# A small U-shaped convolution net on sixteen 32x32 TensorE tiles, with its deconvolutions folded into the convolutions behind them

## The chip, the cores and the metric

The kernel runs on one core of a Trainium2 chip. The metric is the time of one launch in device microseconds, the median of three runs. Engines are called as the profile calls them: PE is TensorE's matmul, PEld its weight load, DVE is VectorE, ACT is ScalarE, POOL is GpSimd, SP is SyncE, whose only work here is to start transfers.

## The reference

`x` is 16 images of 32 channels, 128x128, fp32. Four layers follow, each `x = x + layer(group_norm(x))`; the first three (an attention-like layer, a deformable convolution with a state-space scan, a plain 3x3 convolution) are not touched. The fourth is a small net. Cut to what matters:

```python
y = get_operator(x)                    # five edge filters, 160 channels
y = maxpool2(conv3x3(y, conv1))        # 32 channels from here on; 64x64
y = maxpool2(conv3x3(y, conv2))        # 32x32
y = maxpool2(conv3x3(y, conv3))        # 16x16
y = conv3x3(y, conv4)
y = conv3x3(deconv2x2(y, deconv1), conv5)   # 32x32
y = conv3x3(deconv2x2(y, deconv2), conv6)   # 64x64
y = conv3x3(deconv2x2(y, deconv3), conv7)   # 128x128
return orig * y                             # orig = group_norm(x)
```

`deconv2x2` has stride 2 and a 2x2 kernel, so each input pixel makes a 2x2 block of its own; `conv3x3` pads with zeros and both add a bias. Up to `conv1`'s pooling is the function `edges`; everything behind it, and the product and sum with `x`, is the function `hourglass`, which alone is changed.

## The kernel before

`program` runs its stages one behind the other, each with its own tiles, semaphores and a barrier at its end: norm tables, the layers, `edges` (line names `l3a_`), and last `hourglass` (`l3b_`). `edges` writes `pooled` (32 channels of 64x64) to HBM.

`hourglass` takes four images at a time (`IM`), 32 channels of each, on the 128 partitions; so there are four groups (`NG`), a hardware loop. Weights are block-diagonal 128x128 matrices made on the host (`w_convs`, `w_deconvs`): three quarters of each is zeros. Within a group the layers run strictly in order on PE: `conv2` (8 chunks of 512 columns), `conv3` (2), `conv4` (2), `deconv1`, `conv5` (2), `deconv2` (8), `conv6` (8), `deconv3` (32), `conv7` (32). A convolution chunk is nine matmuls, one for each tap, into one of four PSUM banks (`convolve`, L2200); a deconvolution chunk is one matmul (`spread`, L2207, L2225). ACT adds the bias and scatters a deconvolution's product into the padded input of the next convolution (L2260, L2274); DVE pools (L2316), and for `conv7` multiplies by the normalised `x` and adds `x` (L2343, L2346). The normalised `x` is made by ACT from pieces of eight rows (L2302). Each piece of `x` is loaded by POOL's queue and stored by SP's. SP loads the next group's `in2` when the last `conv2` chunk of this group is done. The memsets of the six padded inputs are on DVE (L2309), and PE waits for all.

Of the kernel before, what the change touches and what calls it, by code (L numbers as in the profile page):

```python
# [5 lines left out]
ACT = mybir.ActivationFunctionType  # L6
ALU = mybir.AluOpType
AX = mybir.AxisListType
P = 128
# [2082 lines left out]
def hourglass(nc, x, table, first, w_convs, w_deconvs, biases, out, B):  # L2092
    IM = P // T
    NG = B // IM
    RO = 8
    NT = H // RO
    XB = 4
    BANKS = 4
    S1, S2, S3 = H // 2, H // 4, H // 8

    phases = (("conv2", S1 * S1 // 512, "v"), ("conv3", S2 * S2 // 512, "v"), ("conv4", 2, "a"), ("deconv1", 2, "a"),
              ("conv5", S2 * S2 // 512, "a"), ("deconv2", 4 * S3 * S3 * 4 // 512, "a"),
              ("conv6", S1 * S1 // 512, "a"), ("deconv3", 4 * S1 * S1 // 512, "a"), ("conv7", H * W // 512, "v"))
    first_chunk, engine_of = {}, []
    for name, n, engine in phases:
        first_chunk[name] = len(engine_of)
        engine_of += [engine] * n
    CHUNKS = len(engine_of)
    assert CHUNKS % BANKS == 0
    PRIMED = CHUNKS  # L2110
    taken_by = {"a": engine_of.count("a"), "v": engine_of.count("v")}

    def chunk_no(g, name, i=0):

        return g * CHUNKS + i + first_chunk[name]

    def taken_before(g, name, engine, i=0):

        return g * taken_by[engine] + i + engine_of[:first_chunk[name]].count(engine)

    with ExitStack() as ctx:
        m = Memory(nc, ctx, "l3b")
        wc = m.sb("wc", [P, 6, 9, P])
        wd = m.sb("wd", [P, 3, 4, P])
        bias = m.sb("bias", [P, 9])
        gn = m.sb("gn", [P, NG, 2])
        gcur = m.sb("gcur", [P, 2])

        in2 = m.sb("in2", [P, S1 + 2, S1 + 2])
        in3 = m.sb("in3", [P, S2 + 2, S2 + 2])  # L2130
        in4 = m.sb("in4", [P, S3 + 2, S3 + 2])
        in5 = m.sb("in5", [P, S2 + 2, S2 + 2])
        in6 = m.sb("in6", [P, S1 + 2, S1 + 2])
        in7 = m.sb("in7", [P, H + 2, W + 2])

        up1 = m.sb("up1", [P, S3, S3])
        up2 = m.sb("up2", [P, S2, S2])
        up3 = m.sb("up3", [P, S1, S1])
        most = m.sb("most", [P, S2, S2])
        xt = m.sb("xt", [P, XB, RO, W])  # L2140
        ht = m.sb("ht", [P, 2, RO, W])
        ps = m.bank("ps", BANKS)
        names = "w_load zeroed in2_load product_done act_took dve_took in3_ready in4_ready gcur_ready h_ready out_ready"
        (w_load, zeroed, in2_load, product_done, act_took, dve_took, in3_ready, in4_ready, gcur_ready, h_ready,
         out_ready) = (m.sem(n) for n in names.split())
        x_in = [m.sem(f"x_in{u}") for u in range(XB)]
        stored = [m.sem(f"stored{u}") for u in range(XB)]
        block = ctx.enter_context(nc.Block())
        group = lambda a: a.rearrange("(g b) c h w -> g (b c) (h w)", b=IM)
        xg, og, fg = group(x), group(out), group(first)  # L2150

        @block.sync
        def _(sp):
            for dst, src in ((wc[:], w_convs), (wd[:], w_deconvs), (bias[:], biases)):
                sp.dma_start(dst, src).then_inc(w_load, 16)
            tb = table.rearrange("(g b) (c q) s -> b c g q s", b=IM, q=4)
            for b in range(IM):
                sp.dma_start(gn[T * b:T * (b + 1), :, :], tb[b, :, :, 0, :]).then_inc(w_load, 16)
            sp.wait_ge(zeroed, 6)
            with sp.Fori(0, NG) as g:  # L2160

                sp.wait_ge(product_done, chunk_no(g, "conv3"))
                sp.dma_start(in2[:, 1:S1 + 1, 1:S1 + 1], fg[at(g), :, :].rearrange("g p (h w) -> (g p) h w", w=S1)).then_inc(in2_load, 16)
                with sp.Fori(0, NT // XB) as j:
                    for u in range(XB):
                        sp.wait_ge(out_ready, g * NT + j * XB + (u + 3))
                        sp.dma_start(og[at(g), :, at(RO * W * (j * XB + u), RO * W)].rearrange("g p n -> (g p) n"),  # L2167
                                     xt[:, u].rearrange("p y x -> p (y x)")).then_inc(stored[u], 16)
            for u in range(XB):
                sp.wait_ge(stored[u], 16 * (NG * NT // XB + 1))  # L2170

        @block.gpsimd
        def _(pool):
            with pool.Fori(0, NG) as g:
                with pool.Fori(0, NT // XB) as j:
                    for u in range(XB):
                        pool.wait_ge(stored[u], (g * (NT // XB) + j) * 16 + 16)
                        pool.dma_start(xt[:, u].rearrange("p y x -> p (y x)"),  # L2178
                                       xg[at(g), :, at(RO * W * (j * XB + u), RO * W)].rearrange("g p n -> (g p) n")).then_inc(x_in[u], 16)

        @block.tensor
        def _(pe):
            pe.wait_ge(w_load, 16 * (3 + IM))
            pe.wait_ge(zeroed, 6)

            def bank_free(g, name, i, u):

                engine = engine_of[first_chunk[name]]
                pe.wait_ge(act_took if engine == "a" else dve_took, taken_before(g, name, engine, i) + (u + 1))  # L2190

            def bank(name, u, n=512):
                first_column = 512 * ((first_chunk[name] + u) % BANKS)
                return ps[:, first_column:first_column + n]

            def convolve(g, name, k, src, size, rows, i, u):

                bank_free(g, name, i, u)
                for tap in range(9):
                    ins = pe.matmul(bank(name, u, rows * size), wc[:, k, tap, :],  # L2200
                                    src[:, at((i + u) * rows + tap // 3, rows), tap % 3:tap % 3 + size], start=tap == 0, stop=tap == 8)
                ins.then_inc(product_done, 1)

            def spread(g, name, k, src, rows, j, tap):

                bank_free(g, name, j * 4, tap)
                pe.matmul(bank(name, tap), wd[:, k, tap, :], src[:, at(j * rows, rows), :], start=True, stop=True).then_inc(product_done, 1)  # L2207

            with pe.Fori(0, NG) as g:
                with pe.Fori(0, S1 // 8 // BANKS) as j:  # L2210
                    pe.wait_ge(in2_load, g * 16 + 16)
                    for u in range(BANKS):
                        convolve(g, "conv2", 0, in2, S1, 512 // S1, j * BANKS, u)
                pe.wait_ge(in3_ready, g + 1)
                for u in range(2):
                    convolve(g, "conv3", 1, in3, S2, 512 // S2, 0, u)
                pe.wait_ge(in4_ready, g + 1)
                for u in range(2):
                    convolve(g, "conv4", 2, in4, S3, S3 // 2, 0, u)

                pe.wait_ge(act_took, taken_before(g, "deconv1", "a") + BANKS)
                for p in range(2):
                    bank_free(g, "deconv1", 0, p)
                    for q in range(2):
                        ins = pe.matmul(bank("deconv1", p)[:, S3 * S3 * q:S3 * S3 * (q + 1)], wd[:, 0, 2 * p + q, :],  # L2225
                                        up1[:, :, :].rearrange("p h w -> p (h w)"), start=True, stop=True)
                    ins.then_inc(product_done, 1)
                pe.wait_ge(act_took, taken_before(g, "conv5", "a") + BANKS)
                for u in range(2):
                    convolve(g, "conv5", 3, in5, S2, 512 // S2, 0, u)  # L2230
                pe.wait_ge(act_took, taken_before(g, "deconv2", "a") + BANKS)
                for j in range(2):
                    for tap in range(4):
                        spread(g, "deconv2", 1, up2, S2 // 2, j, tap)
                with pe.Fori(0, S1 // 8 // BANKS) as j:
                    pe.wait_ge(act_took, taken_before(g, "conv6", "a") + BANKS)
                    for u in range(BANKS):
                        convolve(g, "conv6", 4, in6, S1, 512 // S1, j * BANKS, u)
                with pe.Fori(0, S1 // 8) as j:
                    pe.wait_ge(act_took, taken_before(g, "deconv3", "a") + BANKS)  # L2240
                    for tap in range(4):
                        spread(g, "deconv3", 2, up3, 8, j, tap)
                with pe.Fori(0, H // 4 // BANKS) as j:
                    pe.wait_ge(act_took, taken_before(g, "conv7", "a") + BANKS)
                    for u in range(BANKS):
                        convolve(g, "conv7", 5, in7, W, 512 // W, j * BANKS, u)
# [324 lines left out]
```

## Time and profile before

| | us |
|---|---|
| timed runs | 25,470.23, 25,509.12, 25,365.6; median 25,470.23 |
| span of the profiled execution (the only time recorded of it) | 25,493.9 |
| PE busy in it | 20,717.4, 81% |
| `hourglass`, from the last work of `edges` to the end of the span | 23,568 to 25,494: 1,926 |
| of it before the first matmul | 49 |
| one group of four images | 473 |

The span is cut from the first to the last instruction. Matmuls are pipelined: a record lasts about 165 ns longer than the time until the next one can begin on the same part of the array, so spacings count and not durations.

### The profile page before, as it was taken

What the parts mean: (1) busy time and instruction counts of PE and PEld (TensorE: products, weight loads), DVE (VectorE), ACT (ScalarE), POOL (GpSimd) and SP (SyncE); (2) the same over time, 40 slices, a digit from 0 to 9 for tenths busy, and PEclk for the clock granted to TensorE, in tenths of its full rate; (3) what the DMA queues carried; (4) which work ended last, traced back from release to release, by engine and by line L of the source; (5) the groups of instructions that cost most, each with busy time, mean ns of one, the idle gap of its engine ahead of it and who ended that gap; (6) DMA issues with size and microseconds to landing.
All of it is one profiled execution on the core that took longest, in us unless ns stands there. A gap on an engine that the chain in (4) does not pass through costs nothing. (4 is left out here: it accounts for less than half of the span.)

```text
span 25493.9 us, 384771 instructions
## 1 busy us (share of the span) xinstructions
PE 20717.4 (81%) x134800; PEld 8220.3 (32%) x134800; DVE 15361.5 (60%) x15737; ACT 14120.3 (55%) x22694; POOL 9395.5 (37%) x7816
## 2 busy tenths in 40 slices
PE   6888888884368888888859999997348888888899
PEld 2333333331122222222225444454013333333344
DVE  8999999994167777777835555555133333333111
ACT  6999998994257777777636665665222222222111
POOL 6777777782057777777720010001000000000000
PEclk9999999997678888888877776777679999999999
DMA  1000000006810000000031111112960011001111
GB/s 63 12 12 12 12 12 12 12 12 127 155 47 17 17 18 16 18 18 16 16 79 26 28 33 28 26 28 62 193 149 22 22 29 26 22 22 27 39 38 44
DMA packets 1295345, 995.42 MB, mean 39 GB/s; under 512 B 742248, under 2 KB 1151440, under 8 KB 1258968
## 3 DMA queue, kind: packets, MB, share of 16 engines
q1 hardware_dynamic: 1193416, 849.62, 15.9%
q0 software_dynamic: 26624, 100.67, 1.4%
q10 hardware_dynamic: 74448, 33.14, 0.5%
q8 instruction: 607, 9.95, 0.2%
q14 instruction: 250, 2.05, 0.0%
HBM read 771.60 MB, written 211.63 MB: 39 GB/s over the span
## 5 line engine op out<-in xcount | busy, mean ns | idle before, releaser
L270 DVE TENSOR_TENSOR l_mx<-l_p_v,l_puN 128x2048 f32<-128x2048 f32 x2560 | 5635.2, 2281 | 137.0 <-PE l_p_s L485 124.5
L485 PE MATMUL l_p_s<-l_mx,l_w2z 128*32 128x512 f32 x32768 | 3815.3, 610 | 579.5 <-ACT l_mx L397 307.9
L290 POOL TENSOR_TENSOR l_mx<-l_pv,l_puP 128x2048 f32<-128x2048 f32 x1024 | 3715.5, 3644 | 312.8 <-PE l_p_s L485 307.0
L1196 POOL TENSOR_TENSOR l1m_hc<-l1m_hs,l1m_cs 128x512 f32<-128x512 f32 x2304 | 2923.9, 1269 | 8.5 <-DVE l1m_hs L1148 8.1
L2072 PE MATMUL l3a_p<-l3a_xn,l3a_w 128*128 128x512 f32 (+1 forms) x6144 | 2682.9, 600 | 266.2 <-ACT l3a_xn L1963 266.2
L1148 DVE TENSOR_TENSOR_SCAN l1m_hs<-l1m_da,l1m_carry,l1m_pu 128x512 f32<-128x512 f32 x2304 | 2824.1, 1268 | 106.1 <-ACT l1m_da L1066 2.2
L2178 POOL DMA_DIRECT2D l3b_xt<-x_after x64 | 33.9, 529 | 7634.9 <-DVE l3b_most L2307 5811.9
L1790 ACT ACTIVATE l1d_ab<-l1d_pt 128x1024 f32<-128x1024 f32 x2304 | 2316.1, 1023 | 671.3 <-PE l1d_pt L1552 327.7
L416 ACT ACTIVATE l_mx<-l_pv,l_puP 128x128 f32<-128x128 f32 x8192 | 2446.7, 393 | 0.8
L1668 DVE TENSOR_SCALAR l1d_hat<-l1d_ab 128x1024 f32<-128x1024 f32 x2304 | 1917.0, 833 | 474.0 <-ACT l1d_ab L1790 363.6
L1587 PE MATMUL l1d_po<-l1d_hat,l1d_ring 128*32 128x128 f32 x36864 | 1893.2, 335 | 325.2 <-DVE l1d_hat L1668 214.1
L1138 DVE TENSOR_TENSOR l1m_pu<-l1m_pu,l1m_bs 128x512 f32<-128x512 f32 x2304 | 1476.8, 687 | 1101.0 <-PE l1m_pu L901 1101.0
L397 ACT ACTIVATE l_mx<-l_mx 128x2048 f32<-128x2048 f32 x1024 | 1954.2, 1909 | 52.7 <-POOL l_mx L290 52.1
L485 PEld LDWEIGHTS l_p_s<-l_mx,l_w2z 128*32 128x32 f32 x32768 | 984.2, 112 | 3008.7 <-issue 1745.4
L901 PE MATMUL l1m_pu<-l1m_dts,l1m_sl 32*128 32x512 f32 x4608 | 1417.1, 691 | 479.4 <-ACT l1m_da L1066 469.7
L1066 ACT ACTIVATE l1m_da<-l1m_pr,l1m_an 128x512 f32<-128x512 f32 x2304 | 1457.2, 684 | 565.8 <-PE l1m_pr L894 402.9
L2200 PE MATMUL l3b_ps<-l3b_in,l3b_wc 128*128 (+2 forms) x3888 | 1636.8, 583 | 125.7 <-DMA l3b_in<-pooled 101.0
L2072 PEld LDWEIGHTS l3a_p<-l3a_xn,l3a_w 128*128 128x128 f32 (+1 forms) x6144 | 1096.4, 179 | 1852.7 <-issue 1852.7
L1841 POOL TENSOR_TENSOR l1d_res<-l1d_res,l1d_so 128x2048 f32<-128x2048 f32 x32 | 119.4, 3731 | 4111.4 <-DVE l1d_to L1727 4109.2
L2087 PE MATMUL l3a_pc<-l3a_r,l3a_c 128*32 128x512 f32 x12288 | 1357.0, 604 | 270.6 <-issue 270.6
L1569 PE MATMUL l1d_pg<-l1d_wz,l1d_im 32*128 32x288 f32 x5120 | 1520.3, 677 | 21.9 <-DMA l1d_im<-x_after 9.9
L1587 PEld LDWEIGHTS l1d_po<-l1d_hat,l1d_ring 128*32 128x32 f32 x36864 | 1076.0, 129 | 1297.3 <-issue 864.3
(300 smaller groups left out, 27330.4 us busy)
## 6 DMA issues: line engine op xcount, KB each, us to landing
n_xt<-x_after SPq DMA_DIRECT2D x48, 2048.0 KB
l3a_xb<-x_after SPq DMA_DIRECT2D x352, 256.0 KB, 4.0
l1o_img<-x_after SPq DMA_DIRECT2D x32, 2032.0 KB, 17.5
l_img<-x_after SPq DMA_DIRECT2D x32, 2032.0 KB, 16.9
l1m_sq<-seq SPq DMA_DIRECT2D x256, 144.0 KB
n_xt<-in_x_dram SPq DMA_DIRECT2D x16, 2048.0 KB
l_xs<-in_x_dram SPq DMA_DIRECT2D x128, 256.0 KB, 2.8
x_after<-l_ot SPq DMA_DIRECT2D x128, 256.0 KB, 2.4
```

What stands on the lines that cost most here:

```text
L270: v.tensor_tensor(mx[:, r % QB, :, :, :], columns.unsqueeze(1).broadcast_to([P, 4, G, P]), rows.broadcast_to([P, 4, G, P]), ALU.max).then_ ...
L290: g.tensor_tensor(mx[:, r % QB, :, :, :], pv[:, u, :, :].unsqueeze(1).broadcast_to([P, 4, G, P]), rows.broadcast_to([P, 4, G, P]), ALU.add ...
L397: act.activation(tile, tile, ACT.Relu).then_inc(max_by_g, 1)
L416: ins = act.activation(mx[:, r % QB, q, t, :], pv[:, u, t, :], ACT.Relu, bias=puP[:, u, t, R * q + r:R * q + r + 1])
L485: ins = pe.matmul(p_s[R * q:R * (q + 1), 512 * u:512 * (u + 1)], w2z[:, 31 - r:63 - r], mx[:, r % QB, q, :, :].rearrange("p t v -> p (t v) ...
L1148: dve.tensor_tensor_scan(hs[:, p % 3, part, :], da[:, p % 3, part, :], pu[:, LC * bank:LC * (bank + 1)], carry[:, u, c:c + 1], ALU.mult, A ...
L1196: g.tensor_tensor(hc[:, (3 * u + p) % 6, part, :], hs[:, p % 3, part, :], cs[:, u, :], ALU.mult).then_inc(hc_done, 1)
L1587: ins = pe.matmul(po[C * g:C * (g + 1), 512 * (s % 2):512 * (s % 2) + P], ring[:, (8 * u + s + k) % RING, g, k, :], hat[:, m % 3, n % 2, P ...
L1668: v.tensor_scalar(hat[:, m % 3], ab[:, m % 2], 1.0, 1.0, ALU.min, ALU.subtract).then_inc(hat_done, 1)
L1790: act.activation(ab[:, m % 2].rearrange("p a n -> p (a n)"), pt[:, 1024 * (m % 2):1024 * (m % 2 + 1)], ACT.Abs).then_inc(abs_done, 1)
L2072: ins = pe.matmul(acc[0:n, 512 * (ch % 2):512 * (ch % 2 + 1)], w[:, dx, :], xn[:, k % 2, r:r + RC, dx:dx + W], start=dx == 0, stop=dx == 2)
L2200: ins = pe.matmul(bank(name, u, rows * size), wc[:, k, tap, :], src[:, at((i + u) * rows + tap // 3, rows), tap % 3:tap % 3 + size], start ...
```

## The change

In `hourglass` alone, with the host's layout of its weights:

- The array is used as sixteen tiles of 32x32. Row tile i takes the 32 channels of one image (or strip), column tile k writes one strip (or image). A step of a layer is a "round" of sixteen matmuls, one for each tile, for each tap; a step fills four PSUM banks, and steps take the lower and the upper four in turn. In the small layers between, a layer leaves image and strip swapped, with two or one rows of overlap computed twice.
- `deconv` and the `conv3x3` behind it become one: for each of the four output parities a 2x2 convolution on the small image. Its sixteen 32x32 weights of a level (`wu`) are made by PE before the first group (`prepare`: 216 matmuls), and so is the summed bias (`bu`). Where a folded tap would see the deconvolution's bias behind the border, small matmuls on a constant row (`unfold`) take it away.
- The largest layer (`conv7` with `deconv3`: steps `wide0` to `wide7`) of a group is done among the small layers of the next group, in an order written out for all engines (`chain`). The loop over groups is unrolled: four groups take five turns, `wide` being absent in the first and alone in the last.
- `x` is held for a whole group in two halves (`xs`, 4 MB each in HBM) and updated in place. ACT computes `z` = product times the norm's scale plus a constant, DVE multiplies `(x + less)` by it, and POOL adds the mean at the end of a half. SP stores the half, waits for that, and loads the same half of the next group. POOL also copies the loaded `raw` into the padded `in2`.

```diff
+    chain = ("conv2a", "conv2b", "conv2c", "wide0", "conv3", "wide1", "conv4", "wide2", "up5", "wide3", "wide4",
+             "up6_0", "up6_1", "up6_2", "up6_3", "wide5", "wide6", "wide7")
+        @block.sync
...
+            for g in range(NG):
+                if g + 1 < NG:
+                    sp.wait_ge(in2_ready, g + 1)
+                    sp.dma_start(raw[:].rearrange("p h w -> p (h w)"), fg[g + 1]).then_inc(raw_in, 16)
+                for u in range(2):
+                    sp.wait_ge(finished, 2 * g + u + 1)
+                    sp.dma_start(og[g, u], xs[:, u].rearrange("p s r w -> p s (r w)")).then_inc(stored[u], 16)
+                    sp.wait_ge(stored[u], 16 * (g + 1))
+                    if g + 1 < NG:
+                        sp.dma_start(xs[:, u].rearrange("p s r w -> p s (r w)"), xg[g + 1, u]).then_inc(x_in[u], 16)
+        @block.gpsimd
...
+            def pad(g):
+                pool.wait_ge(raw_in, 16 * (g + 1))
+                if g:
+                    pool.wait_ge(done, number["conv2c", g - 1] + 1)
+                pool.tensor_copy(in2[:, 3:S1 + 3, 1:S1 + 1], raw[:]).then_inc(in2_ready, 1)
+            def finish(g, u):
+                pool.wait_ge(mixed, 8 * g + 4 * u + 4)
+                half = xs[:, u].rearrange("p s r w -> p (s r w)")
+                pool.tensor_scalar(half, half, mean[:, g:g + 1], None, ALU.add).then_inc(finished, 1)
+        @block.tensor
...
+            def free(n):
+                if n >= 2:
+                    ours, count = emptied(n - 2)
+                    pe.wait_ge(dve_took if ours else act_took, count)
+            def conv2(g, part):
...
+                rows = 4 if part == 2 else 8
                 for tap in range(9):
+                    for i in range(IM):
+                        for k in range(S):
+                            r0 = 16 * k + 8 * part + tap // 3
+                            ins = pe.matmul(banks(n)[row(k), i, 0:rows * S1], wc[row(i), 0, tap, :],
+                                            in2[row(i), r0:r0 + rows, tap % 3:tap % 3 + S1],
+                                            start=tap == 0, stop=tap == 8, tile_position=(T * i, T * k))
+            def unfold(l, p, q, dst, src, rows, size, inside, last_tap):
...
+                for i in range(4):
+                    for k in range(4):
+                        pe.matmul(dst(i, k)[:, :, column:column + 1], rim[row(i), l, q, :], bd[row(i), l, 0:rows],
+                                  start=False, stop=False, tile_position=(T * i, T * k))
...
+            def taps_of(l, p, q, dst, src, rows, size, inside):
+                for tap in range(4):
+                    if tap == 3:
+                        unfold(l, p, q, dst, src, rows, size, inside, tap)
+                    for i in range(4):
+                        for k in range(4):
+                            ins = pe.matmul(dst(i, k), wu[row(i), l, 4 * (2 * p + q) + tap, :], src(i, k, tap // 2, q + tap % 2),
+                                            start=tap == 0, stop=tap == 3, tile_position=(T * i, T * k))
...
+        def _(act):
+            def wide(g, j):
...
+                if count >= 2:
+                    act.wait_ge(mixed, count - 1)
+                act.activation(z[:, count % 2, :], ps[:, 512 * base(n):512 * base(n) + 2048], ACT.Identity,
+                               scale=gn[:, g, 0:1], bias=zb[:, g:g + 1]).then_inc(act_took, 1)
...
+        def _(v):
+            def wide(g, j):
...
+                v.wait_ge(act_took, emptied(n)[1])
+                v.wait_ge(x_in[c], 16 * (g + 1))
+                part = xs[:, c, :, p::2, q::2]
+                v.scalar_tensor_tensor(out=part, in0=part, scalar=less[:, g:g + 1],
+                                       in1=z[:, count % 2, :].rearrange("p (s r x) -> p s r x", s=S, x=S1),
+                                       op0=ALU.add, op1=ALU.mult).then_inc(mixed, 1)
+            for turn in range(NG + 1):
+                ahead, behind = turn < NG, turn > 0
+                if ahead:
+                    for part in range(3):
+                        conv2(turn, part)
+                if behind:
+                    wide(turn - 1, 0)
+                if ahead:
+                    conv3(turn)
+                if behind:
+                    for j in range(1, 8):
+                        wide(turn - 1, j)
```

Matmuls of a group, by step: `conv2` 144 + 144 of 512 columns and 144 of 256; `conv3` 144 of 256; `conv4` 144 of 96; `up5` 256 of 64; `up6` 256 of 288; `wide` 512 of 512; and 352 of `unfold`, of 1 to 64 columns. That is 2,096 in place of 1,060.

## Rows read from the trace of the kernel before

**Rows 1.** The page: span, busy time by engine.
```profile
span 25493.9 us, 384771 instructions
PE 20717.4 (81%) x134800; PEld 8220.3 (32%) x134800; DVE 15361.5 (60%) x15737; ACT 14120.3 (55%) x22694; POOL 9395.5 (37%) x7816
```
**Rows 2.** Windows: stretch, us, busy us of each engine, clock, DMA, GB/s.
```profile
core 0: us, PE busy (x) PEld busy (x) DVE busy (x) ACT busy (x) POOL busy (x), PEclk, DMA share, GB/s
23568.00:23617.00 49.00, 0.03 (x3) 0.00 (x0) 25.76 (x17) 0.00 (x0) 2.17 (x4) 0.54 0.58 185
23617.00:24089.00 472.00, 445.67 (x1061) 198.09 (x1061) 51.82 (x61) 57.98 (x72) 8.45 (x16) 0.98 0.12 40
23568.00:25494.00 1926.00, 1784.23 (x4243) 792.72 (x4240) 232.87 (x260) 232.18 (x288) 33.88 (x64) 0.97 0.13 42
```
**Rows 3.** The critical chain of the first group: start, us, what.
```profile
23617.03 63.56 PE l3b_ps L2200 x144
...
23699.19 4.29 PE l3b_ps L2200 x36
...
23795.02 27.74 PE l3b_ps L2207 x64
...
23823.90 247.50 PE l3b_ps L2200 x576
...
24074.69 13.95 DMA l3b_in<-pooled
```
**Rows 4.** Timeline of PE and PEld in `edges`: 128x32 column tiles.
```profile
19159.74 1.48 PE L2087 MATMUL l3a_pc<-l3a_r,l3a_c 128*32 128x512 f32 x12
19160.17 0.13 PEld L2087 LDWEIGHTS l3a_pc<-l3a_r,l3a_c 128*32 128x32 f32 x4 [0.30 <-issue]
```
**Rows 5.** Timeline of PE in the state-space stage: 32x128 row tiles.
```profile
10001.34 0.70 PE L901 MATMUL l1m_pu<-l1m_dts,l1m_sl 32*128 32x512 f32 x2
10001.35 0.70 PE L894 MATMUL l1m_pr<-l1m_dts,l1m_sl 32*128 32x512 f32 x2
10001.87 0.59 PE L901 MATMUL l1m_pu<-l1m_dts,l1m_sl 32*128 32x512 f32 x2
10001.89 0.59 PE L894 MATMUL l1m_pr<-l1m_dts,l1m_sl 32*128 32x512 f32 x2
```
**Rows 6.** Timeline in the deformable stage: sixteen loads and matmuls, four column tiles.
```profile
13302.72 0.38 PEld L1587 LDWEIGHTS l1d_po<-l1d_hat,l1d_ring 128*32 128x32 f32 x16 [0.23 <-issue]
13302.72 0.64 PE L1587 MATMUL l1d_po<-l1d_hat,l1d_ring 128*32 128x128 f32 x16
```
**Rows 7.** Windows of PE alone: the densest long stretch of matmuls.
```profile
17595.90:17631.90 36.00, 34.37 (x504) 1.00 0.02 6
```
**Rows 8.** Instruction fetches of PE, and the branch behind each image of `edges`.
```profile
q8 instruction: 607, 9.95, 0.2%
L2062 PEldq COMPARE_BRANCH  x16: 76/3514/3879, 19235.8 to 23565.4; - x16
```
**Rows 9.** Groups by shape: busy us, mean ns, idle before.
```profile
L397 ACT ACTIVATE l_mx<-l_mx 128x2048 f32<-128x2048 f32 x1024 | 1954.2, 1909 | 52.7 <-POOL l_mx L290 52.1
L2346 DVE TENSOR_TENSOR l3b_xt<-l3b_xt,l3b_ht 128x1024 f32<-128x1024 f32 x64 | 78.4, 1225 | 2.2
L2316 DVE TENSOR_REDUCE l3b_most<-l3b_ps 128x128 f32<-128x512 f32 x40 | 27.7, 692 | 354.3 <-PE l3b_ps L2200 354.3
L290 POOL TENSOR_TENSOR l_mx<-l_pv,l_puP 128x2048 f32<-128x2048 f32 x1024 | 3715.5, 3644 | 312.8 <-PE l_p_s L485 307.0
L277 POOL MEMSET l_sums<- 128x128 f32 x1 | 0.2, 204 | 129.2 <-POOLq L25 129.2
L1172 POOL MEMSET l1m_carry<- 128x36 f32 x1 | 0.1, 127 | 1202.5 <-POOLq L25 1202.5
```
**Rows 10.** Windows, the norm table's loads of 2 MB; and issues to landing.
```profile
5931.00:6036.00 105.00, 0.00 (x0) 0.00 (x0) 72.69 (x120) 0.50 (x1) 0.00 (x0) 0.50 0.85 319
out_dram<-l3b_xt SPq DMA_DIRECT2D x64, 512.0 KB, 2.6
```

More of the change, by code:

```diff
@@ L2094, in hourglass @@
     NG = B // IM
[L2095 to L2098, printed above, removed]
+    S = 4
     S1, S2, S3 = H // 2, H // 4, H // 8
[L2101 to L2107, printed above, removed]
@@ new lines, in hourglass, with emptied @@
+    order = [("prep", 0)]
+    for turn in range(NG + 1):
+        for name in chain:
+            g = turn - 1 if name.startswith("wide") else turn
+            if 0 <= g < NG:
+                order.append((name, g))
+    number = {step: n for n, step in enumerate(order)}
+    by_dve = lambda name: name in ("prep", "conv2a", "conv2b", "conv2c", "conv3")
+    def emptied(n):
+        ours = by_dve(order[n][0])
+        return ours, sum(by_dve(name) == ours for name, g in order[:n + 1])
+    parities = [(p, q) for p in range(2) for q in range(2)]
@@ L2131, in hourglass @@
[L2131 to L2147, printed above, removed]
-        block = ctx.enter_context(nc.Block())
-        group = lambda a: a.rearrange("(g b) c h w -> g (b c) (h w)", b=IM)
-        xg, og, fg = group(x), group(out), group(first)
+        wu = m.sb("wu", [P, 3, 16, T])
@@ L2172, in _ @@
         @block.gpsimd
         def _(pool):
[L2174 to L2179, printed above, removed]
+            pool.memset(in2[:], 0.0).then_inc(zeroed, 1)
@@ new lines, in conv3 @@
+            def conv3(g):
+                n = number["conv3", g]
+                free(n)
+                pe.wait_ge(in3_ready, g + 1)
+                for tap in range(9):
+                    for s in range(S):
+                        for k in range(IM):
+                            ins = pe.matmul(banks(n)[row(k), s, 0:8 * S2], wc[row(s), 1, tap, :],
+                                            in3[row(s), k, tap // 3:tap // 3 + 8, tap % 3:tap % 3 + S2],
+                                            start=tap == 0, stop=tap == 8, tile_position=(T * s, T * k))
+                ins.then_inc(done, 1)
@@ new lines, in conv4 @@
+            def conv4(g):
+                n = number["conv4", g]
+                free(n)
+                pe.wait_ge(in4_ready, g + 1)
+                for tap in range(9):
+                    for i in range(IM):
+                        for k in range(S):
+                            r0 = 4 * k + tap // 3
+                            ins = pe.matmul(banks(n)[row(k), i, 0:6 * S3], wc[row(i), 2, tap, :], in4[row(i), r0:r0 + 6, tap % 3:tap % 3 + S3],
+                                            start=tap == 0, stop=tap == 8, tile_position=(T * i, T * k))
+                ins.then_inc(done, 1)
@@ new lines, in _ @@
+            prepare()
+            for turn in range(NG + 1):
+                ahead, behind = turn < NG, turn > 0
+                if ahead:
+                    pe.wait_ge(in2_ready, turn + 1)
+                    for part in range(3):
[5 more added lines that the diff above has]
+                if behind:
+                    wide(turn - 1, 1)
+                if ahead:
+                    conv4(turn)
+                if behind:
+                    wide(turn - 1, 2)
+                if ahead:
+                    up5(turn)
+                if behind:
+                    wide(turn - 1, 3)
+                    wide(turn - 1, 4)
+                if ahead:
+                    for j in range(4):
+                        up6(turn, j)
+                if behind:
+                    for j in range(5, 8):
+                        wide(turn - 1, j)
@@ L2304, in _ @@
         @block.vector
         def _(v):
[L2306 to L2308 removed]
+            for tile in (in3, in4, in5, in6, bd):
                 v.memset(tile[:], 0.0).then_inc(zeroed, 1)
[L2310 to L2311 removed]
@@ L2349, in program @@
+            for turn in range(NG + 1):
+                ahead, behind = turn < NG, turn > 0
+                if ahead:
+                    for part in range(3):
+                        conv2(turn, part)
+                if behind:
+                    wide(turn - 1, 0)
+                if ahead:
+                    conv3(turn)
+                if behind:
+                    for j in range(1, 8):
+                        wide(turn - 1, j)
 def program(nc, a, out):
```

393 lines of the change are left out of this document (234 added, 159 removed).

## Prediction

> **What bounds the kernel now.** I read the page, then windows over `hourglass`, then its critical chain, then timelines wherever the trace uses part of the array. The reader is to see in the chain that the end is set by PE alone: the last layer is 576 matmuls in 247.5 us, 0.430 us for each 512 columns, and a group of 128 columns per matmul runs at 4.29/36 = 0.119 us; 14 us of each group wait for `in2` [rows 3]. So the stage is worth what PE's matmul count and what replaces PE as the bound leave: new time = 25,494 - 1,926 + S, S being the new stage.
>
> **The array part.** No row shows 32x32 tiles, so their concurrency is put together from two shapes. Column tiles (128x32): twelve matmuls of 512 columns in 1.48 us, three rounds of 0.43 plus the record's tail, four at a time, their four loads starting together in 0.13 us while matmuls run [rows 4]. Four such matmuls read four different streams on all 128 partitions, as much as sixteen tiles will. Row tiles (32x128): four matmuls begin within 0.02 us, the next four 0.53 us later [rows 5]; one behind the other they would need 1.7. Both kinds cost 0.43 a round and not 0.43 a matmul. Bounds for a 16-tile round of 512 columns are 0.43 us (all overlap) and 16 x 0.43 = 6.9 (none); I take 0.43, as both neighbours do. A round of 288 columns is then 0.242, of 256 0.215. For short ones the floor is issue plus a load: I take 0.2 us.
> Per group: `conv2` 9 x (0.43 + 0.43 + 0.215) = 9.7; `conv3` 1.9; `conv4` 9 x 0.2 = 1.8; `up5` 16 x 0.2 = 3.2; `up6` 16 x 0.242 = 3.9; `wide` 32 x 0.43 = 13.8; `unfold` 16 short rounds of sixteen (3.2) and 12 of eight on four tiles, twice each (3.6). Sum 41 us, against 473.
>
> **The issue part.** 2,096 matmuls with a load each are 4,192 instructions. Sixteen pairs begin in 0.38 us, 24 ns a pair, and even that stretch is held by the array (four rounds of 128 columns) [rows 6]; over a long stretch the densest in the trace is 504 in 36 us, 71 ns a pair [rows 7], there among waits for other engines. These are the ends: 24 and 71. I take 26, near the lower, because the upper row is no saturated queue: 54 us for a full turn of 2,096 pairs.
> Unrolled code also has to be fetched: after the branch at the end of an image of `edges` PE waits 3.5 us (median) for instructions, and 607 fetches brought 9.95 MB, 16.4 KB each [rows 8]. The Trainium skill, Runtime: NRT & Kernel Launch, section "Instruction fetch mechanics", says that a fetch is a block of 256 instructions and that crossing a block is mostly hidden. By the page a turn stays at the array's 41 us; by the row's 3.5 us for every block, 16.4 blocks, it is 57. Both lie under the turn worked out next.
>
> **What takes PE's place.** The half-groups of `x`. A half is 4.19 MB; loads run at 319 GB/s [rows 10], so 13.1 us, and I add 2 for start and landing (a 512 KB store needs 2.6 in all [rows 10]): 15 us for a store, 15 for the load, and they are in series by SP's wait for `stored`. Before them POOL adds the mean over 8,192 elements. No row has that form: its memset grows by (204 - 127)/92 = 0.84 ns an element, a two-input operation costs 3,644/2,048 = 1.78 [rows 9], so 6.9 or 14.6 us; one input is nearer the memset, I take 8.5. DVE's update of 2,048 strided elements: 1,225 ns for 1,024 [rows 9] gives 2.4; if the stride doubles it, 4.8. ACT's `z` is 1.9 [rows 9], and eight are 15 us a turn; DVE does 8 x 2.4 plus some 11 of pooling (692 ns for 512 elements [rows 9]), 30 in all. Neither bounds.
> The issues of transfers cost nothing here: POOL's 64 loads (34 us busy in the stage [rows 2]) go, and SP has some 25 in place of 140, most of its time waiting. What is queued behind SP's wait for `in2_ready` is the store of the first half, 40 us later in the turn; behind its wait for `stored` the other half's store, which is where the 4 us of sharing below come from.
> The cycle that closes over the first half of `x`, from one `wide0` update to the next:
> - PE's steps to `wide3`: `conv3`, `wide1`, `conv4`, `wide2`, `up5`, `wide3`, 888 pairs x 26 = 23, and 3 of handovers: 26
> - `wide0`'s own update 2.4, POOL 8.5
> - store 15, load 15, and 4 where the other half's transfers share the engines
> Sum 71 us, above PE's 54. The wait surfaces on DVE, at `x_in` of `wide0`. Queued behind it on DVE is the pooling of `conv3`, for which `conv4` on PE waits, and ACT's third `z`; so for some 10 to 17 us a turn everything stands. That is also where PE's clock may drop.
>
> **Start and end of the stage.** Before: 49 us to the first matmul, 26 of them DVE's memsets [rows 2]. Now POOL clears 4,620 and 9,504 columns, 12 us at 0.84, from about 6 us on; PE then makes the folded weights, 108 matmuls with 128-column loads at 0.119 [rows 3] = 13, and 108 tiny ones, 2.5. `raw` and its copy run beside. First `conv2` at 33. Turn 0 has nothing to fill its gaps: 1,424 pairs x 26 = 37, and 8 of handovers between layers: 78. Turn 1 has its `x` already: `conv2` 11, `wide0`, its update at 96. Then 71 each: 167, 238, 309. In turn 3 `wide7` is mixed at 238 + 26 + 18 (688 pairs) + 4 = 286; POOL 294, store, load and sharing 328; the last four updates 9.4, POOL 8.5, store 15: 361. I add 4 for dips of the clock: S = 365.
> Sum in the profile: 25,494 - 1,926 + 365 = 23,933; that execution lies 24 us above the median of the three runs, so 23,909, said as 23,910: 6.1% faster.
>
> **Rivals.**
> *Transfers bound (the forecast), 84%.* Within it: POOL at 1.78 adds 6 x 4, DVE at double cost 2 to 20, the clock at its lower level throughout makes the array's 41 us a turn 82, 11 over the cycle, some 50 in all, instructions at 35 ns 30. Or the cycle is shorter, if POOL is at 0.84 and transfers overlap well: 60 a turn, S = 330. Own range 310 to 480, with the timed runs' spread of half a per cent: 23,800 to 24,080.
> *Issue bounds, 6%.* If a pair sustained costs the 71 ns of [rows 7], the 8,600 matmuls take 614; with 18 before, 10 between and 28 behind S = 670, time 24,214. For it: no row shows a long run faster. Against: [rows 6], and that those 504 lie between waits. The Trainium skill, TensorE: Matmul & The Clock Gate, section "Wait — 56ns, not 53.3ns?", says that with decoding in the sequencer's program a matmul costs about 62 ns, whatever its size. By that a turn is 130 us where I have 71; the trace's 24 ns speaks against it, though only in a burst.
> *Row and column tiling do not combine, 6%.* If only four of sixteen run together, the array part is 34 x 4 + 7 = 144 a group, S = 650, time 24,194. For it: four row tiles writing four banks while four column tiles write one bank is a pattern nobody shows. Against: each half of it is shown.
> *Slower, 2%.* If in 32x32 tiles each matmul waits for the one before, a group costs 512 x 0.43 + `conv2` 155 + `conv3` 31 + `conv4` 15 + `up5` 27 + `up6` 62 + `unfold` 38 = 548, S = 2,260, time 25,804. It decides where the mean matmul passes 473/2,096 = 0.226 us. Against it [rows 4, 5].
> *Turns overlap less than drawn, 2%:* a wait in the written-out order puts `wide` behind the small layers, 41 + 71 a turn, S = 520.
>
> **How the numbers follow.** The time is the forecast's, 23,910. Its own range holds about 8 in 10 of its 84%, some 70 in all; to leave out no more than 20 the range reaches over the issue and the tiling rivals, 24,214 and 24,194: 23,780 to 24,260. Half a per cent, about 130 us, is what runs of this kernel can tell apart (their spread is 143). Every case but one is faster by far more: faster 0.975, same 0.005, slower 0.02.
>
> **What would show it.** Right: 800 matmuls of 512 columns per full turn, sixteen starting within 0.4 us and again 0.43 later; DVE's longest waits at the `wide0` update on transfers of `x`; wide0-to-wide0 near 71 us; the stage near 365. Wrong: rounds of 1.1 us with gaps put to issue; rounds of 1.7 us with array busy; stores or loads of 4 MB well over 15 us; POOL's add over 15; a granted clock near 0.5, which stretches PE's 54 past 71 and makes it the bound again.

## The result, and the profile after

The changed kernel takes 24,321.44 us (median of four timed runs, 24,311.8 to 24,379.67) where the one before takes 25,468.91: a ratio of 0.9576, 95% interval 0.9543 to 0.9609. So it takes 4.2% less time by that ratio (4.5% between the two medians) at a forecast of 6.1%, and lies 61 us above the upper end of the range, 24,260. The profiled execution has a span of 24,310.2 us. Its last stage, `hourglass`, from the end of the last matmul of `edges` at 23,525.3 to the end of the span, lasts 785 us against 1,926 before and 365 forecast. All that follows is about these 420 us. In the experiments the stage, cut in the same way, is compared and not the whole time: the stages ahead of it, which no kernel here touches, end anywhere between 23,420 and 23,680 in nine of the twelve profiles, a spread as large as what is looked for. The profiles of e1, e3 and e4 are of executions in the program's slower state, in which the stages ahead took some 1,100 us more, while in `hourglass` itself their mean granted clock was 0.78, 0.76 and 0.78 against 0.74 in the changed kernel's, so that their stage is read here; the whole times and ratios given are of other executions of the same kernels. An "idle" of PE is counted below from the start of its last matmul to the start of the next.

The page's line of engines, and its line of PE's instruction fetches; they answer to [rows 1] and [rows 8].
```profile
span 24310.2 us, 406517 instructions
...
PE 19372.3 (80%) x147760; PEld 7736.2 (32%) x147760; DVE 15313.1 (63%) x15589; ACT 13993.1 (58%) x22498; POOL 9563.3 (39%) x7766
...
q8 instruction: 738, 12.09, 0.2%
```
The number of matmul records rises from 134,800 to 147,760, by 12,960. By the forecast's count (2,096 "in place of 1,060") it should have risen by 4 x 1,036 and 216 for `prepare`, 4,360. The columns of [rows 2], again:
```profile
core 0: us, PE busy (x) PEld busy (x) DVE busy (x) ACT busy (x) POOL busy (x), PEclk, DMA share, GB/s
23605.00:23700.00 95.00, 71.56 (x2996) 52.82 (x2982) 14.31 (x23) 9.05 (x15) 3.61 (x1) 0.76 0.02 4
...
23833.00:23893.00 60.00, 7.15 (x175) 4.01 (x184) 0.00 (x0) 0.00 (x0) 23.52 (x2) 0.53 0.43 175
23893.00:24027.00 134.00, 102.79 (x4032) 66.93 (x4020) 45.66 (x22) 25.50 (x23) 21.95 (x2) 0.86 0.17 67
24027.00:24087.00 60.00, 6.95 (x166) 3.71 (x168) 0.00 (x0) 0.00 (x0) 23.62 (x2) 0.53 0.42 175
24087.00:24220.00 133.00, 108.65 (x4197) 71.38 (x4180) 45.53 (x22) 25.58 (x23) 23.11 (x2) 0.86 0.17 67
23524.00:24311.00 787.00, 497.62 (x17215) 344.22 (x17204) 189.20 (x112) 102.19 (x92) 194.18 (x14) 0.74 0.25 101
```
Two things are to be seen. A full turn has some 4,100 matmul records and takes 134 us, 32 ns a record. And between two such turns lie 60 us in which PE does next to nothing while POOL works and 175 GB/s move; this happens twice (idles of 59.7 and 59.2 us). The groups by shape, over the stage:
```profile
L2202 POOL TENSOR_SCALAR l3b_xs<-l3b_xs,l3b_mean 128x8192 f32<-128x8192 f32 x8 | 167.8, 20980 | 428.1 <-DVE l3b_xs L2507 428.1
...
L2507 DVE SCALAR_TENSOR_TENSOR l3b_xs<-l3b_xs,l3b_less,l3b_z 128x2048 f32<-128x2048 f32 x32 | 138.1, 4331 | 233.2 <-ACT l3b_z L2408 212.1 <-DMA l3b_xs<-x_after 21.0
...
L2408 ACT ACTIVATE l3b_z<-l3b_ps,l3b_zb,l3b_gn 128x2048 f32<-128x2048 f32 x32 | 65.9, 2058 | 374.6 <-PE l3b_ps L2301 353.3 <-DVE l3b_xs L2507 21.2
```
POOL's add of the mean takes 20.98 us where the sum had 8.5. The transfer of `x` is waited for once, 21.0 us in all, so transfers are not the bound that the forecast made them. What fills the 60 us is told by the critical chain from the end of a turn to the start of the next:
```profile
23781.04 2.36 DVE l3b_xs L2507
23783.50 21.00 POOL l3b_xs L2202
23804.49 27.39 issue
23831.94 20.98 POOL l3b_xs L2202
23852.94 11.73 DMA out_dram<-l3b_xs
23864.69 0.55 SPq L2186
23865.28 16.86 DMA l3b_raw<-pooled
23882.19 3.62 POOL l3b_in L2197
23885.85 14.15 PE l3b_ps L2250 x356
```
PE waits for a 2 MB load of `raw` that stands on SP's queue behind the store of the second half, which waits for POOL. `raw` itself was free from 23,635 on. And the timelines, first of POOL, then of DVE, show a stall that no dependence explains:
```profile
23783.50 21.00 POOL L2202 TENSOR_SCALAR l3b_xs<-l3b_xs,l3b_mean 128x8192 f32<-128x8192 f32 x1 [147.96 <-DVE l3b_xs L2507]
```
```profile
23785.54 19.38 DVE L2507 SCALAR_TENSOR_TENSOR l3b_xs<-l3b_xs,l3b_less,l3b_z 128x2048 f32<-128x2048 f32 x1 [2.14 <-ACT l3b_z L2408]
23809.81 2.35 DVE L2507 SCALAR_TENSOR_TENSOR l3b_xs<-l3b_xs,l3b_less,l3b_z 128x2048 f32<-128x2048 f32 x1 [4.89 <-ACT l3b_z L2408]
```
The update of the other half needs 2.35 us when POOL is idle, and 19.38 when it starts beside POOL's add: it ends 0.4 us after the add does. Four of the stage's 32 updates are stretched so (19.4 us three times, 13.5 once). The Trainium skill, SBUF — State Buffer, section "Who interferes with whom", has it that these two engines share a pair of ports that one of them holds for a whole instruction; this trace agrees, with these 19.38 us.

### The profile page after: what moved, and what is told of

The parts are those of the page before. It is cut to its first block and busy times, and to the rows that moved or that the text cites. A ratio compares the mean times of both kernels' runs of the same rounds, so it can differ in the third digit from the quotient of the medians.

```text
span 24310.2 us, 406517 instructions
## 1 busy us (share of the span) xinstructions
PE 19372.3 (80%) x147760; PEld 7736.2 (32%) x147760; DVE 15313.1 (63%) x15589; ACT 13993.1 (58%) x22498; POOL 9563.3 (39%) x7766
## 3 DMA queue, kind: packets, MB, share of 16 engines
q8 instruction: 738, 12.09, 0.2%
## 5 line engine op out<-in xcount | busy, mean ns | idle before, releaser
L1655 DVE COPY l1d_ring<-l1d_pg 128x288 f32<-128x288 f32 x1280 | 585.3, 457 | 1455.5 <-PE l1d_pg L1569 1454.9
```

## The experiments

Each started as a theory for a part of the 420 us. Ratios are to the kernel before, run in turn on the same chip. The expectations of e1, e2 and e4 cut the stage at 23,568, where it begins in the profile of the kernel before: by that cut the changed kernel's stage is 742 us, and 43 are to be added to compare with the 785 used here.

**The queues' order.** `e1_raw_load_early` moves one transfer on SP; POOL is left alone.
```diff
+            sp.wait_ge(in2_ready, 1)
+            sp.dma_start(raw[:]..., fg[1]).then_inc(raw_in, 16)
             for g in range(NG):
-                if g + 1 < NG:
-                    sp.wait_ge(in2_ready, g + 1)
-                    sp.dma_start(raw[:]..., fg[g + 1]).then_inc(raw_in, 16)
+                if g + 2 < NG:
+                    sp.wait_ge(in2_ready, g + 2)
+                    sp.dma_start(raw[:]..., fg[g + 2]).then_inc(raw_in, 16)
```

> Only SP's order is changed: the load of raw for the group after next is issued before the stores of the current group, POOL's order stays. Theory A (PE's 60 us of idle before conv2 of groups 2 and 3 are one chain: POOL's add 21, store 11.7, raw's load 17 behind the second half's load, copy 3.6): the load and the store leave the chain, the add and the copy stay in it; about 29 to 31 us less at each of the two places, stage 742 to 682, time about 24,260. Theory B (the transfers' bandwidth sets the turn): the same bytes flow, no change, 24,321.

Measured: stage 736 us (-49), the two idles 30.4 and 29.9 us instead of 59.7 and 59.2; 24,226.95 us, ratio 0.955 (0.948 to 0.962). The load was half of the idles. The stage fell by 49 us and not by the 60 expected, because PE's work between them grew, as the next run shows more clearly.

`e2_raw_and_copy_early` adds the same on POOL, whose queue holds the copy behind both adds:
```diff
             pool.wait_ge(consts_ready, 1)
+            pad(1)
             for g in range(NG):
-                if g + 1 < NG:
-                    pad(g + 1)
+                if g + 2 < NG:
+                    pad(g + 2)
                 finish(g, 0)
                 finish(g, 1)
```

> As the run before, and POOL copies raw into in2 before the adds of the group before. Theory A: the whole 60 us at two places go, less what the next limit gives back; with 134 us of PE work in a turn and x needing 21 + 14 + 15 after wide3, PE is that limit: stage 742 to about 625, time 24,205. Theory B: no change against the kernel after the change.

Measured: stage 685 us (-100), both idles gone; 24,138.12 us, ratio 0.9464 (0.9387 to 0.9541). No instruction and no byte is fewer: 100 us lay in the order of two queues. Expected were 117. From the first matmul of `conv2` to the last of the stage, the idles left out, PE needs 546 us in the changed kernel, 557 in e1 and 567 here. So of 119 us of idle 20 come back as slower work of PE; e7, below, bears on why.

**The add of the mean.** `e3_mean_on_dve` gives POOL's add to DVE and leaves both orders as they were.
```diff
-                finish(g, 0)
-                finish(g, 1)
...
+                if j % 4 == 3:
+                    v.wait_ge(mixed, count + 1)
+                    half = xs[:, c].rearrange("p s r w -> p (s r w)")
+                    v.tensor_scalar(half, half, mean[:, g:g + 1], None, ALU.add).then_inc(finished, 1)
```

> Only the add of the mean is moved from POOL to DVE (one tensor_scalar of 8,192 elements behind the fourth update of a half). If POOL's add is dear by itself (21 us a half) and holds DVE off while it runs (one update took 19.4 us in place of 2.4): DVE's form costs 0.54 ns an element as in the edges stage (8,816 ns for 16,384), 4.4 us; no update is over 3 us; 17 us leave each of the two chains before conv2, 10 to 17 leave the middle of each turn, 25 leave the end: time about 24,240. If DVE's slow update came from the data or from the transfers and not from POOL, it stays near 19 us, and the time falls by the 17 + 17 + 17 of the add alone, 24,270.

Measured: the add takes 4.5 us on DVE, no update is longer than 3, stage 737 us (-48), idles 42.9 and 42.7; 24,245.94 us, ratio 0.9559 (0.9488 to 0.963). So the slow updates came of POOL's add. Of the saving, 17 us came at each idle as expected and 18 at the end (25 expected), and the 10 to 17 expected in the middle of each turn did not come; PE's work took 3 more. The same operation costs 0.55 ns an element on DVE and 2.56 on POOL.

`e4_early_and_dve` is e2 and e3 in one, and the base of all that follows.

> The order of the second run and the add on DVE. If the two waits are all that stands beside PE's own work, PE runs without a gap over 5 us from the first conv2 to the last wide7: 17,151 matmul records at 28 to 29 ns are about 490 us, with 37 before the first and 25 behind the last 550 to 560: time 24,120 to 24,140. If something else limits a turn (transfers of x: store and load 30 us after an add of 4.4), DVE's updates wait for x_in and the time stays above 24,180.

Measured: stage 669 us (-116), with no idle of PE over 5.2 us behind the first matmul; 24,193.78 us, ratio 0.9513 (0.9438 to 0.9588). By the cut used here the expectation was 593 to 603, so the stage missed it by some 70 us. Of e3's 48 only 16 are left here, all of them at the end of the stage (from the start of the last matmul to the end 22.4 us in place of e2's 38.9): with the queues in order, POOL's 21 us lie beside PE's work, which takes the same 567 us in both. These 16 us show in the stage alone; the whole times of e2 and e4 don't tell the two apart. The expectation had PE at 28 to 29 ns a record and nothing else; the trace has 34, in one piece. Nor does DVE wait for transfers of `x`, the expectation's other case. PE itself had to be explained.

**What PE waits for.** Of PE's waits in e4 behind the first matmul, 9.4 us are for other engines and 109 for nothing that the profile shows ("issue"). The critical chain of e4, in a stretch of small matmuls with no transfer:
```profile
25060.16 0.18 PE l3b_ps L2291
25060.35 1.81 PE l3b_ps L2302 x109
25062.16 1.48 issue
25063.63 0.22 PE l3b_ps L2302
25063.86 0.39 PE l3b_ps L2285 x23
25064.24 0.16 PE l3b_ps L2291 x4
25064.40 1.18 PE l3b_ps L2302 x70
25065.58 1.52 issue
25067.11 0.85 PE l3b_ps L2302 x41
...
25069.04 1.81 issue
25070.85 4.48 PE l3b_ps L2302 x54
```
109 matmuls with their loads take 1.81 us, 17 ns each; then PE stands 1.5 us. It starts again every 3.5 to 3.7 us. In the stage's fetch records (one for each 16.4 KB, 12.09 MB / 738) the same distance is found: median 3.70 us where nothing else moves. A fetch brings some 256 instructions (e8, below, shows 254), or 128 pairs, so 29 ns a pair. The same chain where `x` and `raw` are being loaded:
```profile
24991.87 4.73 PE l3b_ps L2251 x129
24996.59 1.96 issue
24998.55 4.02 PE l3b_ps L2251 x104
25002.58 1.64 issue
25004.22 2.74 PE l3b_ps L2251 x117
25006.96 3.47 issue
25010.43 4.05 PE l3b_ps L2251 x128
25014.48 1.89 issue
```
Now it starts again after 5.7 and 6.2 us. Over the stage, some 32 of 130 fetch intervals lie beside transfers, with a median near 6 us. The fetches and the pauses also keep step. Over e4's 67 pauses of more than 0.9 us behind the first 100 us of the stage, PE starts again 2.4 us (median) after a fetch's packet starts, alone as well as beside transfers, and the packet takes 1.0 us in both. What grows is the time from PE's start to the start of the next fetch's packet: 1.1 us alone, 3.3 beside transfers. So the theory: PE is bound by its instruction fetches, and large transfers slow these. Rivals: the array, the clock, waits for other engines. Four kernels, one after the other on one chip, each run once:

`e5_half_columns` halves the columns of the middle taps (7 of 9, and 2 of 4 in the folded layers), which takes some 30% of the array's columns away and keeps the instructions. The edit of `conv2`; `conv3` and the folded layers have the same:
```diff
-                            ins = pe.matmul(banks(n)[row(k), i, 0:rows * S1], wc[row(i), 0, tap, :],
-                                            in2[row(i), r0:r0 + rows, tap % 3:tap % 3 + S1],
+                            some = rows // 2 if 0 < tap < 8 else rows
+                            ins = pe.matmul(banks(n)[row(k), i, 0:some * S1], wc[row(i), 0, tap, :],
+                                            in2[row(i), r0:r0 + some, tap % 3:tap % 3 + S1],
```

> e4 with half the rows (so half the columns) in the middle taps of every step: taps 1 to 7 of the 3x3 convolutions conv2 and conv3, taps 1 and 2 of the folded ones; the number of matmuls stays, and the output is no longer the reference's. Theory (the instructions bound TensorE: blocks of 128 load-and-matmul pairs are fetched one behind the other, about 3.7 us each): a turn stays within 5 us of e4's 144, stage 645 to 675 us. Rival (the array bounds it, 512 columns twice for fp32): a turn loses about 40 us, stage about 510 us.

Measured: stage 664 us (-5), a full turn 141 us against e4's 145. The array does not bind the turn. Where rounds are of 512 columns it did: `conv2a` of group 2 went from 9.2 to 7.5 us; the steps behind gave most of that back.

`e6_no_unfold` takes 2,816 records with next to no columns away (`if False` before the call of `unfold`):

> e4 without the 352 source matmuls a group that take the bias back at the rims (they have 1 to 32 columns; 704 records of 4,192); left out of the computation. Theory (instruction fetch bounds TensorE, 29 ns a pair): 20 us less a turn, stage about 587 us. Rival (columns through the array bound it): these have next to no columns, 3 to 5 us less a turn, stage about 652 us.

Measured: stage 592 us (-77). 2,816 pairs, 27 ns each: matmuls of 1 to 64 columns cost what a fetch costs.

`e7_quarter_transfers` moves one of the four strips in each store of `x`, and in each load behind the first group's:
```diff
-                    sp.dma_start(og[g, u], xs[:, u]...).then_inc(stored[u], 16)
+                    sp.dma_start(og[g, u][:, 0:1], xs[:, u, 0:1]...).then_inc(stored[u], 16)
...
-                        sp.dma_start(xs[:, u]..., xg[g + 1, u]).then_inc(x_in[u], 16)
+                        sp.dma_start(xs[:, u, 0:1]..., xg[g + 1, u][:, 0:1]).then_inc(x_in[u], 16)
```

> e4 with a quarter of the bytes in each store and load of x after the first group's load (one of the four strips; the rest of the output isn't written). Theory (fetches of instructions go at 3.7 us a block alone and at about 5.9 us beside these transfers, 32 of them in e4): 32 x 2.2 us = 70 us less, minus what the quarter still takes, stage 600 to 620 us. Rival (the slow steps come of the clock, which falls there, or of waits on the drain): stage 655 to 670 us.

Measured: stage 609 us (-60). Eight of them lie behind the last matmul (14.5 us from its start to the end, where e4 has 22.4), since the last store is shorter; the others are PE's, 515 us in place of 567. The windows of the same steps (`conv2b`, `conv2c` of group 2), first in e4, then in e7:
```profile
24992.00:25016.00 24.00, 15.41 (x523) 9.76 (x493) 4.25 (x5) 0.00 (x0) 0.00 (x0) 0.93 0.86 347
```
```profile
23983.00:24001.50 18.50, 15.03 (x564) 10.44 (x554) 5.73 (x5) 0.00 (x0) 0.00 (x0) 1.00 0.59 230
```
46 ns a record beside 347 GB/s, 33 beside 230. The clock (0.93 against 1.00) can't make 13 ns a record: at 0.93 PE's 15.41 busy us would shrink by 1.

`e8_bf16_operands` asks for the number of records: the operands of the main loop's matmuls become one constant bf16 tile.
```diff
-  pe.matmul(dst(i, k), wu[row(i), l, 4 * (2 * p + q) + tap, :], src(i, k, tap // 2, q + tap % 2), ...
+  pe.matmul(dst(i, k), wb[row(i), :], mb[row(i), 0:rows * size].rearrange("p (y x) -> p y x", x=size), ...
```

> e4 with both operands of every main-loop matmul a constant bf16 tile (output is not the reference's; prepare stays fp32). Theory (an fp32 matmul is issued as two loads and two matmuls, a bf16 one as one of each; the issue of pairs bounds): 2,096 records a group instead of 4,192, a turn of 65 to 80 us, stage 390 to 430 us, near the 365 of the forecast that counted 2,096. Rival (the record count doesn't depend on the type): 4,192 records, turn 130 to 145 us, stage above 620 us.

Measured: stage 413 us. The window over its stage, and its fetches:
```profile
23511.00:23925.00 414.00, 217.94 (x8828) 167.33 (x8820) 163.69 (x120) 100.54 (x92) 26.88 (x8) 0.54 0.47 189
```
```profile
q8 instruction: 672, 11.01, 0.2%
```
8,828 records for 17,215, 66 fetches fewer than e4's 738 (16,768 instructions fewer, 254 for each), and 256 us less than e4: 30.5 ns for each pair that is gone, where e6 had 27. The type changes the array's work as well, so e8 alone would not say which of the two counts; e5 and e6 do. The mean clock was 0.54: TensorE was near its lower level, 1.2 GHz, for nearly the whole stage. A full turn takes 79 us (71 forecast).

**The start.** The timeline of `prepare` in the changed kernel:
```profile
23549.19 46.25 PE L2227 MATMUL l3b_ps<-l3b_wc,l3b_wd 32*128 32x32 f32 x216 [23.88 <-DVE l3b_rim L2447]
23595.37 9.46 PE L2232 MATMUL l3b_ps<-l3b_bias,l3b_wc 32*32 32x1 f32 x213
```
214 ns for 32 columns, at a granted clock of 0.50, all in one row tile. `e9_prepare_in_rows`, run once, lets each of the three folded layers use its own row tile and bank (`wd` is laid out three times, layer innermost):
```diff
-      pe.matmul(ps[:, first_column:first_column + T], wd[0:T, l, 2 * a + b, :], wc[0:T, 3 + l, 3 * dy + dx, :], ...)
+      for l in range(3):
+          pe.matmul(ps[:, first_column:first_column + T], wd[row(l), l, 2 * a + b, :], wc[row(l), 3 + l, 3 * dy + dx, :],
+                    ..., tile_position=(T * l, 0))
```

> e4 with the folding of the weights (216 records at 213 ns each, one behind the other in one row tile, 46 of prepare's 55.6 us) done in three row tiles at once, one for each folded layer, each writing its own bank. Theory (row tiles run beside each other here too): these 46 us become 15 to 20, stage 669 - 28 = 635 to 645 us. Rival (a load of 128 columns holds up the other row tiles, or the clock of 0.50 is the price): prepare stays over 45 us, stage 660 to 675 us.

Measured: stage 642.5 us (-26.5), and the same 216 records in 15.58 us, a third. `conv2` starts 30.7 us sooner; some 4 of these were lost again behind it:
```profile
23444.87 15.58 PE L2228 MATMUL l3b_ps<-l3b_wc,l3b_wd 32*128 32x32 f32 x216 [23.90 <-DVE l3b_rim L2448]
```
`e10_all` has all of it (e2's orders, the mean on DVE, e9's row tiles) and starts `prepare` without waiting for memsets and rim sums.

> e9, and prepare doesn't wait for the memsets and the rim sums (only for the weights; the wait stands behind it): all of the mends together (raw and copy early, mean added by DVE, prepare in three row tiles and at once). Theory (terms of the stage add): prepare begins 3 to 8 us sooner, stage 627 to 642 us against after's 785, so the kernel about 145 to 155 us under after's 24,321: 24,170 us, ratio to before 0.949 (0.945 to 0.953). Rival (prepare's gain is eaten by the start of conv2, which waits for the first copy at 22 us, or by later fetches): stage 660 us, 24,200 us.

Measured, the median of six executions: 24,153.23 us (24,095.15 to 24,245.12), ratio 0.9475 (0.9439 to 0.951); stage 640.5 us. That is 5.2% under the kernel before. Its stage is the shortest of the versions with the reference's whole work, 144 us under the changed kernel's; by whole times, with a spread of 150 us, it can't be told from e2's 24,138.12. The early start brought 2.6 us, not 3 to 8: the first matmul came 21.3 us into the stage in place of 23.9, and of e9's 642.5 just 2 went. Its term was too large; the rest held.

## Why the prediction went wrong, point by point

The stage was forecast at 365 us and took 785. The experiments split it:

| | us | from |
|---|---|---|
| each fp32 matmul issued twice | 256 | 669 - 413, e4 and e8 |
| order of SP's and POOL's queues | 100 | 785 - 685, e2 |
| POOL's add, as far as it shows | 16 | 685 - 669, e4 |
| start: `conv2` at 79.3 and not 33 | 46 | the trace; 26.5 of it taken back by e9 |
| left over | 2 | 420 less the rest |

The order in which they are taken matters: e3 alone took 48 us, and behind e2 it is 16. That the rows leave only 2 us is luck. It says that e8 needs 333 us from the first `conv2` to the end where the forecast had 365 - 33 = 332; but the forecast had transfers of `x` as the bound there, and in e8 DVE waits for them 13.5 us in all, while PE waits 123 us for issue and 13 for other engines.

- **"2,096 matmuls with a load each are 4,192 instructions": the step that failed.** An fp32 matmul is two records, with two loads. The rows said so: 576 matmuls for `conv7` in [rows 3], where the source has 32 chunks of nine, and x1061 in [rows 2] for a group of 530 in the source. The count for the new kernel was taken from the source, the one for the kernel before from the trace, and they were set side by side. The rate of 26 ns is one per record; the right sum is 4,192 pairs a turn, 109 us. e8, in which the count is as forecast, gives 413, inside the forecast's own 310 to 480.
- **The rate of 26 ns itself was nearly right, for a reason that was weighed and dropped.** PE does 17 ns a pair in a burst; what sets the pace is a fetch of 128 pairs every 3.7 us, 29 ns. [Rows 8] had those 3.5 us. The prediction worked out that every block would cost as much and called it harmless, since with half the instructions it lay under the transfers' cycle. At 4,192 pairs it is 16.4 x 2 blocks x 3.7 = 121 us a turn, of 134 measured. For the rest there are transfers beside the last steps of a turn, and `conv2`, whose rounds of 512 columns take 29 to 32 ns a record; how it divides was not measured. The Trainium skill, Runtime: NRT & Kernel Launch, section "Instruction fetch mechanics", has crossing a block mostly hidden, since instructions are issued more slowly than they arrive. Here a block is used up in 128 x 17 ns = 2.2 us and the next needs 3.7, so it is not hidden, and the measurement decides.
- **The array part: combining held, the sum didn't.** Sixteen tiles do run together. A window in `conv2`, all of 512 columns:
```profile
23616.00:23626.00 10.00, 10.00 (x341) 8.28 (x310) 3.01 (x4) 0.00 (x0) 0.00 (x0) 1.00 0.01 3
```
  341 matmuls and 310 loads in 10 us are 29 to 32 ns a record, sixteen in 0.47 to 0.52 us, near the 0.43 forecast and far from 6.9. But each source matmul needs two rounds, so the part is about 82 us a turn and not 41. e5 shows that it doesn't bind even so.
- **"POOL 8.5": 21.0.** The nearest row was chosen by the number of inputs (a memset, 0.84 ns an element); the operation costs 2.56, above the two-input row's 1.78 that was the upper bound. Neither bound held.
- **The cycle over the halves of `x`: not the bound.** Its parts were store 15 (measured 11.7 and 13.5), load 15 (13.9), update 2.4 (2.35), `z` 1.9 (2.06): all fair. It didn't close because PE is slower; with half the records, in e8, it surfaced for 13.5 us. The wait on `x_in` was 21.0 us once, not 10 to 17 a turn.
- **A step that was not there: what stands behind a waiting instruction on SP and on POOL.** The prediction named the stores behind SP's waits, and not the load of `raw` behind them nor the copy behind POOL's adds. That is 100 us, and would have been a wait at any rate of PE.
- **The start: 13 us for the folded weights, measured 46.2.** 108 matmuls at 0.119 us is again the source's count, at the upper clock; 216 records at 0.214 with a clock of 0.50 is what ran.
- **The rivals.** "Issue bounds" (6%, S = 670) names what happened, with the wrong row behind it: 71 ns for a pair, where it is 29 ns a record and two for each matmul. e4, in which nothing but issue is left, comes to 669, which is a coincidence of the sizes; so is the rival's turn of 130 us beside the 134 measured, since a pair takes 17 ns in a burst. "Tiling does not combine" is refuted by the 29 ns above, and by e9. "Slower" is refuted by the result, and "less overlap" left no trace in PE's waits.
- **Why the stages ahead don't matter.** They end 43 us sooner in this profile than in [rows 2] and are the same code: that is the spread of runs. With it the profile's own sum is 25,494 - 1,926 - 43 + 785 = 24,310.

What stays open: why a fetch's packet starts later beside transfers (shared engines, queues, or memory), since only the amount was changed; what the granted clock is worth in this stage, since no run changed it alone; and what the real kernel would give with bf16 operands in full, as e8's are constants. A version without `unfold`'s 2,816 records that still takes the bias back, on ACT for example, was not tried; e6 prices it at up to 77 us.

## What to carry to other kernels

Count instructions in the trace, for a kernel's existing shapes, before multiplying a rate by a count from the source: in fp32 one matmul here is two. When an array is cut into small tiles, price the instruction stream first, block by block of 128 pairs, and add what large transfers take from its fetches. For each wait that is added to a queue, write down everything that stands behind it, loads for the group after next included; that list was worth 100 us here without an instruction less.

## What the runs showed of the hardware that was not expected

- PE's stream of loads and matmuls is fed at one 16.4 KB block per 3.7 us (median in e4's stage without transfers), and per some 6 us beside transfers at 347 GB/s; a burst inside a block runs at 17 ns a pair. The block's own packet takes 1.0 us either way; it is its start that comes later.
- A tensor-scalar add of 128x8192 fp32 takes 20.98 us on POOL, 4.5 us on DVE; a copy of 128x4096 on POOL 3.61 us, 0.88 ns an element. So POOL's price could not be told from the number of inputs.
- DVE's update, which reads two operands in SBUF, stands still until POOL's add ends if it starts beside it: 19.38 us in place of 2.35, and 2.35 each time once DVE does the add (e3).
- Three row tiles of 32x128 with 32 columns each run fully beside each other: 216 records in 46.25 us in one, in 15.58 in three, both at a clock of 0.50.
- With bf16 operands in place of fp32, and so half the records, the mean granted clock fell from 0.78 (e4) to 0.54, and the stage was shorter all the same by 256 us. The array's work fell too, so this doesn't price the clock by itself.
